# A decoder layer with 32 experts: the first normalisation and the running sums of chosen experts in another form of VectorE instruction

## The reference

```
x = layernorm(x + self_attention(x))           # 16 heads of 64
x = layernorm(x + cross_attention(ctx, ctx, x, mask))   # one head of 64
x = layernorm(x + experts(x))                  # 32 experts, top 8, capacity 512

layernorm(x) = (x - mean) / sqrt(var + 1e-5)

# experts
probs = softmax(x @ gate.T); topw, topi = top_k(probs, 8); topw /= topw.sum()
pos   = running count of each expert over all tokens in order   # a place in its buffer
buf[e, pos] = token                            # dropped where pos >= 512
out   = sum over the 8 of topw * down_e(silu(gate_e(x)) * up_e(x))
```

## Time and profile before

| | us |
|---|---|
| median of the runs | 2260.1 |
| the profiled execution, whole | 2263.32 |
| its span, first to last instruction | 2261.5 |
| PE busy | 2058.9 (91%) |
| DVE busy | 1365.9 (60%) |
| ACT busy | 1195.7 (53%) |
| POOL busy | 1103.0 (49%) |
| mean granted clock of PE | 0.954 |

### The profile page before, as it was taken

The page is one execution under the profiler, slowest core; times in us unless marked ns, Lnnn a source line. Parts: engine busy times, 40 slices in busy tenths (PEclk is TensorE's granted clock), DMA queues, the critical chain, the costliest instruction groups (busy, mean ns, idle before and its releaser), DMA issues.

```text
span 2261.5 us, 43549 instructions
## 1 busy us (share of the span) xinstructions
PE 2058.9 (91%) x15590; PEld 1257.2 (56%) x15590; DVE 1365.9 (60%) x2409; ACT 1195.7 (53%) x2878; POOL 1103.0 (49%) x863
## 2 busy tenths in 40 slices
PE   7898988988998998998998866999999999999990
PEld 5566666666666666666666643444444444444440
DVE  5557577677677667767757764554555455545544
ACT  6765665665665666566566532344434443444334
POOL 3454454454554454545445422555554555455522
PEclk9899999999999999999999977999999999999995
DMA  6121011011011101101101113677777777777739
GB/s 202 37 72 46 27 35 53 19 37 47 19 52 33 35 35 33 38 32 33 51 19 33 42 34 131 169 200 177 173 171 203 173 173 173 205 171 171 176 42 315
DMA packets 114600, 219.74 MB, mean 97 GB/s; under 512 B 14576, under 2 KB 37104, under 8 KB 114544
## 3 DMA queue, kind: packets, MB, share of 16 engines
q1 hardware_dynamic: 85600, 148.73, 18.9%
q0 software_dynamic: 28944, 70.27, 16.8%
HBM read 158.67 MB, written 60.29 MB: 97 GB/s over the span
## 4 chain that ended last, share of the span: by engine, by line
PE 70%; DVE 14%; issue 7%; ACT 6%; POOL 1%; DMA 1%; DVEq 0%; ACTq 0%; SPq 0%; POOLq 0%
PE bank L474 46%; PE bank L784 11%; PE bank L538 4%; ACT arena_p L859 3%; PE bank L550 3%; PE bank L773 3%; DVE s_max L1118 2%; PE bank L512 2%; DVE stage L1285 2%; DVE x L1165 2%; PE bank L668 1%; DVE stage L1287 1%; ACT arena_wo L1078 1%; POOL arena_p L1533 1%; DVE code L1291 1%
## 5 line engine op out<-in xcount | busy, mean ns | idle before, releaser
L474 PE MATMUL bank<-arena_v,arena_wo 128*128 128x512 f16 x2304 | 502.5, 379 | 0.7 <-PE bank L675 0.7
L1533 POOL TENSOR_TENSOR arena_p<-arena_p,s_rden 128x1024 f32<-128x1024 f32 x128 | 246.0, 1922 | 428.7 <-DVE s_rden L1126 428.7
L474 PE MATMUL bank<-xt,arena_wo 128*128 128x256 f16 x3072 | 378.9, 283 | 3.8 <-DVE arena_wo L1088 3.7
L474 PEld LDWEIGHTS bank<-arena_v,arena_wo 128*128 128x128 f16 x2304 | 225.4, 98 | 273.1 <-PE bank L675 1.5
L1633 POOL DMA_INDIRECT acc_rows<-arena_wo,cur_to x128 | 202.1, 1579 | 310.0 <-ACT arena_wo L1058 278.7
L859 ACT ACTIVATE arena_p<-bank,s_neg 128x256 f32<-128x256 f32 x512 | 235.4, 472 | 204.1 <-DVE s_neg L1121 204.1
L474 PEld LDWEIGHTS bank<-xt,arena_wo 128*128 128x128 f16 x3072 | 301.0, 101 | 75.1 <-issue 30.0
L1088 DVE SCALAR_TENSOR_TENSOR arena_wo<-stage,arena_wo 128x3072 f16<-128x3072 f32 (+2 forms) x74 | 182.3, 2465 | 183.8 <-ACT arena_wo L931 169.0
L784 PE MATMUL bank<-arena_wo 128*128 128x512 f16 x1152 | 264.2, 379 | 0.7 <-DVE arena_wo L1475 0.7
L1088 DVE SCALAR_TENSOR_TENSOR arena_v<-bank,arena_v 128x512 f16<-128x512 f32 x192 | 129.5, 688 | 194.9 <-ACT arena_v L869 104.1
L1627 POOL DMA_INDIRECT arena_p<-x_rows,cur_from x128 | 216.9, 1695 | 56.4 <-issue 29.3
(11 more groups left out here) (159 smaller groups left out, 3051.8 us busy)
## 6 DMA issues: line engine op xcount, KB each, us to landing
stage<-wguT SPq DMA_DIRECT2D x32, 1536.0 KB
stage<-wdnT SPq DMA_DIRECT2D x32, 768.0 KB
xt<-xT SPq DMA_DIRECT2D x16, 512.0 KB, 4.0
xr<-x_rows SPq DMA_DIRECT2D x16, 512.0 KB, 4.0
stage<-ctxT SPq DMA_DIRECT2D x16, 512.0 KB, 4.6
x_rows<-x SPq DMA_DIRECT2D x16, 512.0 KB, 2.8
acc_rows<-x SPq DMA_DIRECT2D x16, 512.0 KB, 3.7
arena_wo<-acc_rows SPq DMA_DIRECT2D x8, 1024.0 KB, 10.8
```

The lines of the kernel that those rows point to most:

```text
L474: mm = pe.matmul(out_ap, lhs(a, i), rhs(c, i), start=(n == 0 and i == 0), stop=(n == 2 and i == chunks - 1))
L1533: gp.tensor_tensor(rows, rows, s_rden[:, j % 2, :].unsqueeze(2).to_broadcast([P, 4, S]), ALU.mult)\
```

## The change

The two instructions of `norm1` become scalar-tensor-tensor instructions: the mean stays a per-partition scalar, `rstd1` becomes a second tensor source, one value per partition repeated 512 times. The two additions into `sel_sum` become scalar-tensor-tensor instructions that compare `left` (float32) with -1 and add the result to the other half of `sel_sum`, so they no longer read `sel`; `sel` itself is still made, at the same place. The waits, the increments and the order of the instructions stay.

```diff
@@ norm1 @@
-                    vec.tensor_scalar(x1[:, t, :], z[:, t, :], mv1[:, t, 0:1], rstd1[:, t:t + 1],
-                                      ALU.subtract, ALU.mult).then_inc(x1_done, 1)
+                    vec.scalar_tensor_tensor(out=x1[:, t, :], in0=z[:, t, :], scalar=mv1[:, t, 0:1],
+                                             in1=rstd1[:, t:t + 1].to_broadcast([P, D]),
+                                             op0=ALU.subtract, op1=ALU.mult).then_inc(x1_done, 1)
@@ choose @@
                 step(b, 10)
-                vec.tensor_tensor(sel_sum[:, 1, :], sel_sum[:, 0, :], sel[:, 0, :], ALU.add).then_inc(rt, 1)
+                vec.scalar_tensor_tensor(out=sel_sum[:, 1, :], in0=left[:, 0, :], scalar=-1.0, in1=sel_sum[:, 0, :],
+                                         op0=ALU.is_equal, op1=ALU.add).then_inc(rt, 1)
@@ places @@
-                vec.tensor_tensor(sel_sum[:, 0, :], sel_sum[:, 1, :], sel[:, 1, :], ALU.add).then_inc(rt, 1)
+                vec.scalar_tensor_tensor(out=sel_sum[:, 0, :], in0=left[:, 1, :], scalar=-1.0, in1=sel_sum[:, 1, :],
+                                         op0=ALU.is_equal, op1=ALU.add).then_inc(rt, 1)
```

## The result

The changed kernel takes 2273.4 us (median, 2270.10 to 2274.22) against 2259.8 of the kernel before in the same comparison: ratio 1.0055, 95% interval 1.0038 to 1.0073. Run again with more executions it took 2271.5 against 2260.3, ratio 1.0050, interval 1.0038 to 1.0062, that is 8.6 to 14.0 us slower. 2269.9 was forecast, with 2264 to 2276 around it.

What follows compares the result with a forecast made beforehand. DVE, waiting in turn with POOL, was taken to set the pace from `norm1` to the round's end. Longer passes gave 8.8 us, the clock +1: 9.8 on 2260.1, so 2269.9 us, range 2264 to 2276.

Steps and rivals of the forecast that it cites:

- The new form waits for POOL as the old ones do: At L1165 and L1259: scalar-tensor-tensor still waits for POOL's instruction, then does its pass; L1259 still waits the same 2 us.
- The row of `xt`: Scalar-tensor-tensor on `xt` in `low`, float32 source: ends 1.09 us after POOL's L1538, taken as evidence the form waits.
- It holds POOL back too: At `norm1`: the longer first L1165 holds POOL's L1533, which ends 0.27 us later (at least 0.14).
- rival A: Scalar-tensor-tensor waits for POOL but does not hold it; L1533 takes 1.89, about -5 us, 2255; chance 5%.
- The pass is twice as long: At `norm1`: the new form's pass over 512 elements takes 0.54 to 0.55 us instead of 0.29.
- my two prices of 0.69 and 0.82: First L1165 in the new form: lower price 0.69 us without per-partition scalar, upper 0.82; sums 6.6 or 8.8 us.
- The sums cost 0.02 each, one of them covered: Additions at L1259 and L1272: each +0.02 us; in the loop L1272's is covered by DVE's 0.30 us idle for ACT.
- my 0.53 for the normalisation: At `norm1`: the second L1165 ends 0.53 us later each round, at 1110.22 against 1109.69; 0.40 at the lower price.
- Nothing hides it: Between DVE and PE: no slack absorbs the delay; the contrary case, 2260 within 0.2%, had chance 5%.
- The clock: PE in the loop: two or three second low clock stretches in place of one, +1 us; bounds -0.8 and +9.6.
- Rival C: Second low clock stretch in half the rounds or more: +5 to +9 on top of 8.8, 2274 to 2279; chance 12%.
- The sum: Whole kernel: 8.8 us from the longer instructions plus 1 for the clock, 9.8 us in all.

Runs made afterwards that it cites:

- half_pass: Changed kernel with the first normalisation over 256 of 512 columns only, the other columns left zero; ratio 0.9996 to the kernel before.
- norm_only: Kernel before with only the two instructions of the first normalisation in the new form, the sums as before; ratio 1.0049.
- sums_only: Kernel before with only the two additions into `sel_sum` in the new form, the normalisation as before; ratio 0.9995.
- late_bias_warm: Kernel before with POOL's 128x1024 sum moved to the end of step 7, plus 12 and 28 filling matrix products in PE's idle times; 2249.8 us, ratio 0.9960.
- late_bias: Kernel before with POOL's 128x1024 sum moved from the end of step 5 to the end of step 7; ratio 0.9981.
- norm_first: Kernel before with the normalisation put ahead of the reciprocals that release POOL's 128x1024 product; ratio 0.9999.
- both: Kernel before with POOL's sum moved to the end of step 7 and the normalisation put ahead of the reciprocals; ratio 0.9994.

## Why the prediction was right

**The new form waits for POOL as the old ones do.** Right, in both places: 0.56 after POOL's product and 0.04 after its sum. The row of `xt` was the one that told it.

**It holds POOL back too** (rival A denied it). Right: the product beside the first new instruction takes 2.36 us and ends 1.74 after it.

**The pass is twice as long.** Right, and shown alone by half_pass and norm_only. The size was a little off: the first instruction takes 0.75 us, between my two prices of 0.69 and 0.82, of which I took the upper. One per-partition scalar costs some 0.06 over none, not as much as two. So the two instructions are 0.47 longer and not 0.53. The plain rounds of norm_only are 0.52 longer all the same (82.54 on average for 82.02). In the changed kernel 0.49 of it are there when PE reaches L484 (21.06 us from the start of the normalisation, for 20.57); the few hundredths behind that are not placed.

**The sums cost 0.02 each, one of them covered.** Not settled: a plain round of sums_only is 0.04 longer than before on average (82.06 for 82.02), more than I had counted, but the changed kernel's plain rounds, 82.55, are hardly longer than norm_only's 82.54. These are hundredths, from one profile each. A plain round is 0.53 longer for my 0.55; that it came so close is in part luck, since 0.06 of my 0.53 for the normalisation were not there and about as much came from elsewhere.

**Nothing hides it.** Right: PE's first idle time takes all of it, 4.23 for 3.72.

**The clock.** I put +1 for two or three second low stretches in place of one; there were three in place of one, +1.6, in both profiles. The place, some 22 us behind the normalisation, and the price, 0.8, were as in the round of 82.84. The number was a guess between none and all thirteen, and that it held is luck: norm_only has four, and what starts these stretches is open. (Rival C adds up to 2278 at its upper end, 8.8 and 9 above 2260.1, not to 2279.)

**The sum.** 9.8 us; the profiled loop shows 8.5, round 1 0.5, and the pair of round 16 takes 1.41 for 1.00, which makes 9.4. The runs give 11.3 (8.6 to 14.0). The profiled executions differ by only 6.8: all that comes after the loop took 3.2 us less in that pair, of which 2.1 lie in round 15, and the time up to round 1 took 0.9 more. What lies between 9.4 and 11.3 is inside the interval; the drain differs by several us between executions (64.4 to 68.9 us for round 15 in the fourteen profiles), with the clock in it, and I cannot say whether the change shifts its mean.

## What to carry to other kernels

When a short VectorE instruction takes as long as a GpSimd instruction beside it and ends with it, rewriting it in another form with two SBUF sources bought nothing here: compare the ends of the two, and look for any row of the new form beside GpSimd before trying it. Moving the GpSimd instruction away is no sure gain either: in late_bias_warm the 2 us came back at a two-element instruction that takes 0.17 us in the kernel before, so look at every VectorE instruction that will start beside its new place. A form that loses the faster pass pays on both engines, since each holds the other. And in a loop whose engine clock drops in its idle times, a shorter chain may bring idleness to a place where the slow clock costs more; look at where the low stretch falls in the round before and after, and judge a gain with the clock kept up as well, checking that the filling has not changed which instructions meet.

## What the runs showed of the hardware that was not expected

Three different kernels (late_bias, norm_first, both) settle at rounds of 81.93, 81.94 and 81.93 us, although the first saved 2.0 us of its chain and the second hardly any. In each the low stretch of PE's clock then stays at one place in the round, 17, 7 and 18 us behind the normalisation. With products that keep the clock at 1.00, the first and the last of them take 81.20 and 81.04, although a VectorE instruction then waits 2 us more. So late_bias and both seem to run in step with the clock, and small savings do not show in them. For norm_first this is not shown: no run kept its clock up, its low stretch lies where it cost the kernel before nothing, and PE's first wait is 3.61 us for 3.72, which may be all of its gain.

A float16 tensor-tensor, a float32 tensor-tensor, a tensor-scalar and a scalar-tensor-tensor all end at a fixed distance behind the GpSimd instruction that they meet, about as long as their own pass over the elements: 0.03 us for 2, 0.04 for 32, 0.09 for 64, 0.28 for 512 in tensor-scalar, 0.56 for 512 and 1.09 for 1024 in scalar-tensor-tensor.
